# Last block of an eight-block kernel: roots as powers on POOL, another layout of the scan, another order of its pieces

## The reference

```
x = x + ffn(layernorm(x)); x = x + scan(layernorm(x)); x = x + ffn(layernorm(x))

ffn(x):   h = silu(x @ w_gate) * (x @ w_up)        # 256 -> 1024
          of each group of 4 values of h keep the 2 of largest |h|
          return h_kept @ w_down                    # 1024 -> 256
scan(x):  ct = concat(x shifted by one step, x)
          re, im = sigmoid(relu(ct @ W_act.T))      # 128 complex channels
          m = cummax(sqrt(re*re + im*im), over time)
          kv = associative_scan(complex product, (re/m, im/m))
          return (kv @ W_val.T) * sigmoid(relu(ct @ W_rec.T)) ** 4
```

## Time and profile before

| | us |
|---|---|
| three runs | 1676.60, 1682.62, 1684.93 |
| the profiled execution's own time | 1681.59 |
| its span | 1679.8 |
| DVE busy | 1075.5 (64%) |
| PE busy | 1409.5 (84%) |
| ACT busy | 617.2 (37%) |
| POOL busy | 285.7 (17%) |

### The profile page before, as it was taken

One profiled execution on the slowest core, in us unless ns is written; L12 is line 12 of the kernel. 1 busy time (PEld: TensorE's weight loads), 2 busy tenths in 40 slices (PEclk: granted clock), 3 DMA queues, 4 the chain that ended last, 5 costly groups with the idle time before them and its releaser, 6 DMA issues. The chain is left out here.

```text
span 1679.8 us, 21713 instructions
## 1 busy us (share of the span) xinstructions
PE 1409.5 (84%) x8144; PEld 1004.7 (60%) x8144; DVE 1075.5 (64%) x2163; ACT 617.2 (37%) x1144; POOL 285.7 (17%) x239
## 2 busy tenths in 40 slices
PE   2799999867999877799966899988579977979698
PEld 2455555456888756688864334433258765766576
DVE  5555454176877456778837566566267688787875
ACT  1254544333333222333321565656522422333221
POOL 1210000034433201233331330200120101011000
PEclk9799897678999988899986999999989998989899
DMA  8715320040000000000024421300000000000000
GB/s 179 97 31 67 53 26 1 1 146 1 1 1 1 1 0 1 1 1 1 1 59 51 86 54 33 48 2 1 1 1 1 1 0 1 1 1 0 13 13 25
DMA packets 23064, 42.01 MB, mean 25 GB/s; under 512 B 4705, under 2 KB 6497, under 8 KB 22833
## 3 DMA queue, kind: packets, MB, share of 16 engines
q1 hardware_dynamic: 22960, 40.64, 13.2%
HBM read 14.54 MB, written 2.10 MB: 10 GB/s over the span
## 5 line engine op out<-in xcount | busy, mean ns | idle before, releaser
L1285 DVE TENSOR_REDUCE attn_negm<-ps 128x2 f32<-128x1024 f32 (+3 forms) x256 | 256.1, 1021 | 124.1 <-PE ps L923 66.3
L1133 ACT ACTIVATE attn_probs<-ps 128x512 f32<-128x512 f32 (+3 forms) x512 | 237.0, 515 | 200.6 <-PE ps L946 124.4
L453 POOL TENSOR_TENSOR moe_h_low<-moe_h,moe_h_high 128x512 fp32r<-128x512 f32 x96 | 137.0, 1429 | 331.7 <-ACT moe_h_high L403 331.7
L937 PE MATMUL ps<-attn_qs,attn_ks 64*128 64x512 f32 (+3 forms) x512 | 156.9, 426 | 37.9 <-ACT attn_probs L1133 35.6
L1645 PE MATMUL ps<-sb_f_down,tail_h 128*128 128x256 f32 x512 | 129.8, 401 | 56.8 <-DVE x L1915 41.1
L1645 PEld LDWEIGHTS ps<-sb_f_down,tail_h 128*128 128x128 f32 x512 | 101.2, 200 | 78.1 <-DVE x L1915 44.1
L913 PE MATMUL ps<-attn_ks,attn_qs 63*128 63x512 f32 (+3 forms) x512 | 122.0, 473 | 29.3 <-DMA attn_ks<-attn_part_low 24.3
L420 ACT ACTIVATE moe_silu<-ps 128x512 f32<-128x512 f32 x96 | 57.4, 598 | 228.6 <-PE ps L326 228.5
L937 PEld LDWEIGHTS ps<-attn_qs,attn_ks 64*128 64x128 f32 x512 | 73.8, 198 | 102.2 <-ACT attn_probs L1133 96.7
L961 PE MATMUL ps<-attn_probs,attn_va 128*32 128x512 f32 (+3 forms) x1024 | 128.9, 580 | 0.0
L913 PEld LDWEIGHTS ps<-attn_ks,attn_qs 63*128 63x128 f32 x512 | 52.8, 202 | 97.8 <-issue 67.0
(11 more groups left out here) (317 smaller groups left out, 3282.8 us busy)
## 6 DMA issues: line engine op xcount, KB each, us to landing
attn_qs<-attn_part_high SPq DMA_DIRECT2D x64, 128.0 KB, 5.1
attn_qs<-attn_part_low SPq DMA_DIRECT2D x32, 128.0 KB, 4.7
attn_ks<-attn_part_high SPq DMA_DIRECT2D x32, 128.0 KB, 6.4
...
x<-in_x SPq DMA_DIRECT2D x1, 1536.0 KB, 11.1
attn_qs<-attn_mT SPq DMA_DIRECT2D x64, 4.0 KB
...
```

What stands on the lines that cost most here:

```text
L453: pool.tensor_tensor(hc.low[:, j % RING, :], h[:, j % RING, :], hc.high[:, j % RING, :], ALU.subtract).then_inc(low_done, 1)
L937: last = pe.matmul(ps[:, SC + k, 0:width2(kt)], ks[e:e + ROWS2, b % 2, key_tile(hd), kt * P:(kt + 1) * P], qs[e:e + ROWS2, b % 2, hd // 2, ...
L1133: act.activation(pr[:, s2 % RING, j, 0:n], ps[:, SC + k, 0:n], ACT.Exp, scale=HD ** -0.5).then_inc(exp_done, 1)
L1285: dve.tensor_reduce(m, ps[:, 2 * half:2 * half + 2, 0:width1(qt)], AX, ALU.max, negate=True).then_inc(r1_free, 1)
```

## The change

- The norms of the last block, but for the first sequence's, lose the Newton steps and the negated mean: `moments` ends at var + eps, and `normalise` on POOL raises it to -0.5 (`ALU.pow` with a tile of -0.5) and subtracts the mean.
- ACT's root and DVE's reciprocal go. DVE takes the running maximum of the squared magnitude, and POOL's `invert` raises its 128x512 values to -0.5.
- The scan buffer is [place in the segment, segment]: levels and tree steps read contiguously, the division reads at a stride of 8, `fill` writes at a stride of 8 into a second buffer `zt` in the order of time, and ACT copies into it what `fill` doesn't write (`totals`).
- ACT copies the down sums of a pass to `dsum` (`down_sum`), in the slot before; down waits for that copy, and DVE adds from SBUF in one instruction, behind product and selection of its slot.
- The value of a sequence is added to x in one instruction, at place 13.
- Pieces stand in other slots. POOL's four weight subtractions wait for the first norm.

```diff
+def moments(dve, c, x, tiles, nb, done):
+    for k, t in enumerate(tiles):
+        c.do(dve.bn_stats(nb.stats[:, k, :], x[:, t, :]))
+    c.hold()
+    for k in range(len(tiles)):
+        c.do(dve.bn_aggr(nb.mv[:, k, :], nb.stats[:, k, :]))
+    c.sync()
+    c.end()
+    dve.tensor_scalar(nb.var[:, :], nb.mv[:, :, 1], EPS, None, ALU.add).then_inc(done, 1)
...
+    for p in range(PASSES):
+        act_at[added(p) - 1].append(("sum", p))
+        dve_at[added(p)].append(("add", p))
...
-        pe_at[s + 3].append(("act", b, 0))
-        pe_at[s + 4].append(("act", b, 1))
-        act_at[s + 3].append(("act", b, 0))
-        act_at[s + 4] += [("act", b, 1), ("square", b)]
-        dve_at[s + 5].append(("sum", b))
-        act_at[s + 6].append(("root", b))
-        dve_at[s + 6].append(("peak", b))
-        dve_at[s + 7] += [("divide", b)] + [("level", b, i) for i in (1, 2, 3)]
-        dve_at[s + 8] += [("level", b, i) for i in (4, 5, 6, 7)]
-        dve_at[s + 9] += [("tree", b, d) for d in TREE[:3]]
-        dve_at[s + 10] += [("tree", b, d) for d in TREE[3:]]
+        pe_at[s + 3] += [("act", b, 0), ("act", b, 1)]
+        act_at[s + 3] += [("act", b, 0), ("act", b, 1), ("square", b)]
+        dve_at[s + 4] += [("sum", b), ("peak", b)]
+        pool_at[s + 4].append(("invert", b))
+        dve_at[s + 5] += [("divide", b)]
+        dve_at[s + 6] += [("level", b, i) for i in (1, 2, 3)]
+        dve_at[s + 7] += [("level", b, i) for i in (4, 5, 6)]
+        dve_at[s + 8] += [("level", b, 7)] + [("tree", b, d) for d in TREE[:2]]
+        dve_at[s + 9] += [("tree", b, d) for d in TREE[2:4]]
+        dve_at[s + 10] += [("tree", b, d) for d in TREE[4:]]
         dve_at[s + 11].append(("fill", b))
-        pe_at[s + 6].append(("rec", b, 0))
-        act_at[s + 6].append(("rec", b, 0))
-        pe_at[s + 8].append(("rec", b, 1))
-        act_at[s + 8].append(("rec", b, 1))
+        act_at[s + 11].append(("totals", b))
+        pe_at[s + 5].append(("rec", b, 0))
+        act_at[s + 5].append(("rec", b, 0))
+        pe_at[s + 7].append(("rec", b, 1))
+        act_at[s + 7].append(("rec", b, 1))
         pe_at[s + 12] += [("out", b, m) for m in range(2)]
-        dve_at[s + 12] += [("out", b, m) for m in range(2)]
+        dve_at[s + 13].append(("out", b))
...
-                    at_least(pe, x_done, p)
+                    at_least(pe, sum_done, p)
...
+            def down_sum(p):
+                act.wait_ge(down_done, FC * (p + 1))
+                at_least(act, x_done, p)
+                act.activation(dsum[:, :, :], ps[:, DOWN:DOWN + 2, :], ACT.Copy).then_inc(sum_done, 1)
...
+                cn.step(pool.tensor_tensor(n.y[:, c0:c0 + NT], n.var[:, c0:c0 + NT], power[:, 0:NT], ALU.pow))
...
+            def invert(b):
+                pool.wait_ge(peak_ready, b + 1)
+                pool.tensor_tensor(sq[:, 0, :], sq[:, 1, :], power[:, :], ALU.pow).then_inc(inverted, 1)
...
+            pool.wait_ge(xn_ready["f"], 1)
             for k, (n, at) in enumerate(parts):
                 pool.wait_ge(w_high, k + 1)
...
             def add_to_x(p):
-                dve.wait_ge(down_done, FC * (p + 1))
-                for k in range(2):
-                    t0 = NT * (p % B) + 2 * k
-                    xk = x[:, t0:t0 + 2, :]
-                    last = dve.tensor_tensor(xk, xk, ps[:, DOWN + k, :].rearrange("p (t d) -> p t d", t=2), ALU.add)
-                last.then_inc(x_done, 1)
+                dve.wait_ge(sum_done, p + 1)
+                xb = x[:, NT * (p % B):NT * (p % B + 1), :]
+                dve.tensor_tensor(xb, xb, dsum[:, :, :].rearrange("p k (t d) -> p (k t) d", t=2), ALU.add).then_inc(x_done, 1)
```

More of the change, by code:

```diff
@@ L1686, in square @@
                 act.activation(sq[:, :, :], z[:, :, :], ACT.Square, bias=halfone[:, 1:2]).then_inc(sq_ready, 1)
-            def root(b):
-                act.wait_ge(sum_ready, b + 1)
-                act.activation(sq[:, 1, :], sq[:, 0, :], ACT.Sqrt).then_inc(mag_ready, 1)
             def rec_gate(b, m):
@@ L1709, in do @@
                     row(*a)
+                elif kind == "sum":
+                    down_sum(*a)
+                elif kind == "totals":
+                    totals(*a)
                 elif kind == "act":
@@ L1713, in do @@
                     square(*a)
-                elif kind == "root":
-                    root(*a)
                 elif kind == "rec":
@@ L1800, in peak, with multiply @@
             def peak(b):
-                cp.start(b)
-                dve.wait_ge(mag_ready, b + 1)
-                cp.step(dve.tensor_tensor_scan(sq[:, 0, :], sq[:, 1, :], sq[:, 1, :], 0.0, ALU.max, ALU.max))
-                cp.step(dve.reciprocal(sq[:, 1, :], sq[:, 0, :]))
-                cp.end()
-            def divide(b):
-                if b > 0:
-                    dve.wait_ge(ready, jobs.number[("out", b - 1, 1)])
-                dve.scalar_tensor_tensor(zz[:, :, :], z[:, :, :], 1.0, sq[:, 1, :].unsqueeze(1).broadcast_to([P, 2, T]),
-                                         ALU.add, ALU.mult).then_inc(divided, 1)
+                dve.wait_ge(sum_ready, b + 1)
+                dve.tensor_tensor_scan(sq[:, 1, :], sq[:, 0, :], sq[:, 0, :], 0.0, ALU.max, ALU.max).then_inc(peak_ready, 1)
+            def divide(b):
+                at_least(dve, totals_done, b)
+                dve.wait_ge(inverted, b + 1)
+                inverse = sq[:, 0, :].rearrange("p (n s) -> p s n", s=S1)
+                for k in range(2):
+                    last = dve.scalar_tensor_tensor(zz[:, k, :, :], z[:, k, :].rearrange("p (n s) -> p s n", s=S1), 1.0, inverse,
+                                                    ALU.add, ALU.mult)
+                last.then_inc(divided, 1)
                 cx.start(b)
                 dve.wait_ge(divided, b + 1)
-            def multiply(part, carry, shape):
+            def multiply(part, carry, shape, product=None):
+                product = product or part
                 n = int(np.prod(shape))
```

117 lines of the change are left out of this document (71 added, 46 removed).

## The result

| | before | after |
|---|---|---|
| median of all runs, us | 1683.78 (1676.6 to 1689.07) | 1961.72 (1958.22 to 1963.55) |
| span of the profiled execution | 1679.8 | 1958.6 |
| mean granted clock | 0.91 | 0.849 |

A forecast was written before the change was run, and what follows sets the result against it. In the last block PE and DVE wait for each other; afterwards PE bounds, with turns of 58.3 (55.1 + 2.0 + 1.2) against 71.4. Gains at start, stalls, three turns and last stretch, less 1.1, total 62.0: 1620 us, range 1606 to 1650.

The forecast's parts named there:

- The large power: POOL's 128x512 power: taken as 7.4 us, between 1.27 and 14.0; up to 6.2 free, so 1.2 a turn.
- Rival (b): POOL's large power value by value, DVE shut out: decides from 23 us; a power of 40 gives 1752; chance 0.11.
- The lock-out: DVE's comparisons, having two SBUF inputs, cannot run beside POOL's large power and start as it ends, at 41.6 in the turn.
- POOL's rows: POOL's four normalised rows for the scan: 2.16 us alone or 4.41 beside DVE's two-input work; 2.0 a turn charged.
- The gates at places 5 and 7: PE's recurrent gate matmuls in a turn: counted as 2 x 3.45 us within PE's need of 55.1.
- Rival (c): PE's waits move: small power has a 1 to 2 us start-up, SiLU delayed; turns 62 to 64, 1636 us; chance 0.13.
- The heap: DVE's work ahead of the selection PE needs: done at 61.1, wanted at 59.9, so a wait of 1.2 a turn.
- The last stretch: End of the last block: 6 us gained, with PE expected to wait 6 for DVE in the fill and the row.
- the long wait for the addition: PE's 11.06 us wait at a turn's end for DVE's addition to x: replaced by ACT's copy, priced at zero.
- The start: Start of the last block: POOL's splits behind DVE's first norm, PE's first chunk at about 1220.5, gain 6.1 us.
- Slot 3: PE's stall at 1240.13 goes with DVE's twelve small steps: 2.31 and 1.3 for the low clock, 3.6 us.
- rival (e): The scan's contiguous layout gives nothing, small steps being bound by a fixed 0.17: DVE at 52, no change in time.

The follow-up runs named there:

- e9: The kernel after, with the large power over the first 64 of 512 columns and the constant 0.3 for the other 448; 1677.16 us, one run.
- e1: The kernel after, with ACT's square root and DVE's reciprocal back in place of the large power; 1693.46 us, ratio 1.0107.
- e2: e1, with DVE negating the mean again and POOL adding it instead of subtracting; small powers stay; 1676.63 us, ratio 0.9984.
- e5: e2, with the recurrent gates back at places 6 and 8 instead of 5 and 7; 1653.79 us, ratio 0.9797.
- e10: e6, with DVE's reciprocal at place 4, behind the running maximum, instead of place 5; 1629.66 us, ratio 0.9701.
- e6: e5, with the scan's statistics directly behind the addition, ahead of the level and tree steps of place 8; 1649.91 us, ratio 0.9799.
- e11: e10, with the levels of the scan one place later; 1628.22 us, ratio 0.9695.

## Why the prediction failed, step by step

Row f stands for the normalised rows of the second feed-forward.

| kernel | turn, us | PE waits in it for | us |
|---|---|---|---|
| before | 71.4 | addition to x; filled scan | 11.06; 1.49 |
| after | 143.1 | row f; row of scan; two banks | 67.92; 7.07; 3.43, 2.73 |
| e9, power of 64 columns | 75.3 | row of scan; two banks | 7.08; 3.43, 3.40 |
| e1, no large power | 75.8 to 77.8 | row of scan; two banks | 7.07; 3.43, 4.47 to 6.06 |
| e2, and addition on POOL | 73.7 | row of scan; two banks | 4.23; 3.43, 6.13 |
| e5, and gates later | 64.3 | selection; row of scan | 6.29; 1.40 |
| e10, and reciprocal early | 58.8 | row f | 2.42 |
| forecast | 58.3 | row of scan; selection | 2.0; 1.2 |

**The large power.** The step that failed is "POOL is 1.27/0.68 = 1.87 times slower than DVE, which gives 7.4". It took 82.2, eleven times as much: the ratio of two elementwise operations, put on a root and a reciprocal that run on other engines, says nothing of a power. The upper bound of 14.0 was no bound: it took the power to be made of passes at POOL's elementwise price, and no row had a function on POOL. Rival (b) named this mechanism and the break-even of 23 us, and got 0.11. Its formula gives 1620 + 4 x 74.8 = 1919 at 82.2; the measured 1962 is more, and the order did not give its 1620 either (e9: 1677). That a quantity without a row has an open upper end was written in the rival, and was not in the chance.

**What waits behind the power.** The prediction followed only the consumer, the division. It missed POOL's own queue: the small power and the rows f stand behind the large one, and from the second turn on these, not the division, stop PE (67.92 at 1543.09).

**The lock-out.** The comparisons were to start when the power ends. They ran inside it at their full speed, under 82 us in the kernel after and under 10.6 in e9. The 2.26 beside POOL's subtraction was real, but belongs to POOL's elementwise operations and not to a power. The rule of the Trainium skill (SBUF — State Buffer, the section SBUF: two separate sides) that the lock is held for the whole instruction does not agree with the trace for a power: a lock held for 82.18 us would leave no room for comparisons that start 5.3 us into it. The other way round there is a stretch: in e10 the small power takes 2.95 beside DVE's division for 1.01.

**POOL's rows.** "2.16 alone or 4.41 beside DVE's two-input work" was carried over to the new form at no cost. Subtract in place of add is one word of the diff and more than doubles them where DVE leaves them alone (4.83 for 2.17). This costs 16.8 us by the medians of e1 and e2.

**The gates at places 5 and 7.** The prediction counted their matmuls and not their banks. It priced moved instructions by their own time, while what moved was which earlier job must have freed the bank. The two waits and the low clock are worth 23 to 28 us (e2 to e5). Rival (c), which got 0.13, said that the waits move and put it at 1636; it named neither the subtraction nor the banks. Its start-up of 1 to 2 us for the small power is not measured by itself: the whole small power takes 1.01 alone and 2.95 beside the division. The order shown ahead of the prediction has the comparisons (L1949) in front of the value's product (L1908), whose bank the gate of that very place needs.

**The heap.** The reckoning for the selection let the division start behind the statistics and found a wait of 1.2. In e5 and e6 it is 6.3, with the reciprocal's 3.35 back in the heap; e10 takes those out, and the turn is 58.8. So this step was right in kind. That the turn meets the 58.3 is partly luck: it has no wait for the scan row (2.0 forecast) and none for the selection (1.2), but 2.42 for row f, which the prediction did not have.

**The last stretch.** From the first down projection behind the third long wait (1563.61 before) to the end of the span are 116.2 us. The prediction took 6 off and added 1.1 for the copy, which gives 111.3. In e10 it is 119.5 (1515.52 to 1635.0), with waits of 2.50, 5.30 and 3.83, about as much as before. The wait of 6 that the prediction put in place of today's had no row behind it, and the gain did not come; where the other 3 us went was not followed.

**Right.** PE does not wait for the copy (1.02 us, mean of eight in the kernel after), and the long wait for the addition is gone. The scan's operations are 0.29 and 0.22 where 0.30 and 0.23 follow from the forecast; the division 2.08 for 2.1. The start: from DVE's first statistics of the block to PE's first chunk 1205.64 to 1216.30 = 10.7, where it was 1209.83 to 1226.62 = 16.8, so 6.1, as forecast. Slot 3 no longer stalls. Eight of nine table loads are gone. DVE's turn is 50.24 for 48.7, PE's need 54.99 (e11) for 55.1. Whether the scan's layout gives anything (rival (e)) was not tried by itself.

**The forecast of 1620.** e11, with the root back on ACT, the addition on POOL, the gates at their old places, the statistics first and the reciprocal early, is at 1628, or 1632 by its ratio to the kernel before. In the block itself the miss is larger: from PE's first chunk to the end the forecast comes to 453.2 less 55.9 (its 62.0 without the start's 6.1), which is 397.3 us, and e10 and e11 take 413.6 and 415.1. About half of this difference lies in the last stretch. The reading of PE's and DVE's work was sound, and the order that was handed to them was not checked against it. e10 and e11 are not told apart; they are the best versions here, 3% faster than the kernel before.
